# Attention steps for two heads at a time, diagonal blocks turned in two halves, and elementwise work on POOL

## The chip, the cores and the metric

The kernel runs on one core of a Trainium2 chip. The metric is the device time of one execution in microseconds (us). Before the change the median of three runs is 7115.45 us (7112.15 to 7116.17).

Engines are named as in the profile: PE (matmuls; PEld is its weight load), DVE and ACT (elementwise work and reductions, both read PSUM), POOL (elementwise work in SBUF, and indirect DMAs) and SP (which issues most DMAs). Each engine works through its own queue in order; semaphores tie the queues together.

## The reference, cut to what matters

```python
x = x + 0.5 * ffn(layernorm(x))       # mixture of 8 experts, top 2, on 16 x 1024 tokens of width 256
x = x + attn(layernorm(x))
x = x + 0.5 * ffn(layernorm(x))

def attn(x):                          # 16 batches, S = 1024, 16 heads of 16
    q = x @ W_q
    latent = (x @ W_k + x @ W_v) @ W_down_kv
    k, v = latent @ W_up_k, latent @ W_up_v
    scores = einsum('bhqd,bhkd->bhqk', q, k) / 16 * exp(-0.01 * abs(i - j))
    return (softmax(scores) @ v) @ W_o
```

## The kernel before, in words

The program is one expert layer (m1), the attention, and a second expert layer (m2). Only the attention (`class Attention`) is changed, so the functions of `Moe` stay as they are.

The attention takes 16 batches of 16 heads. Two heads make a pair (128 pairs, 8 per batch). A pair's scores are 1024 queries by 1024 keys for each head, and they are computed twice. First with queries on the partitions: `scores` (L933) fills half of four PSUM banks, `ps`, with 128 x 1024 scores of one head, and DVE takes the row maxima (L1193). The diagonal blocks need another decay, so at one place in eight (`DIAG`) DVE multiplies them by `Dm` into `Sd` instead (L1189), and a `fold` (L1198) takes their maxima. `max` (L1203, L1208) joins both into `m`, which goes through PE (`mturn`, L1004), ACT (L1097, L1098), POOL (`mlo`, L1261) and two DMAs through DRAM (`msend`, L900, L904) into two extra rows of `qst`. POOL subtracts `m` from `Sd` (`sub`, L1256). Then the scores come a second time with keys on the partitions and the maximum already subtracted, a row-tile (128 keys) at a time: `turned` (L945) fills the two halves of the queries, all but the diagonal block, and a transposition of `Sd` (L1033) fills that block. Each half is one PSUM unit of 128 x 512, in one of three banks (4 to 6) that all such units share in rotation; ACT takes the exponential into `P` (L1117), and `W` (L1049) multiplies it by V into bank 7, for four units at once in four column groups of the array. `P` has 8 slots, that is two row-tiles of both heads.

The operands of L933 and L945 are 48 and 50 rows high, head 0 on partitions 0 and up, head 1 on 64 and up. Score pieces of one head and turned pieces of the other are issued alternately, so that the two halves of the array work side by side. The transposition L1033 uses all 128 rows.

`order` writes the sequence in which all engines work. A step is one head of one row-tile; scores run ahead of the turned ones by one pair and `LEAD` steps. Between the steps it places the work of two lists: `late` (`norm`, `share`, and at a batch's end `oturn`, `out`, `sum`) and `ahead`, the next batch's preparation: `gather` (8 indirect DMAs, L1238), `add` (gate times expert row plus residual, L1146), `keep`, `stats`, `newton`, `center` (L1178), `turn`, `latent`, then 8 times `project` (L989, L992), `scale` (POOL L1245), `hi` (ACT L1088), `lo` (POOL L1250), `send` (two DMAs of `hl` to DRAM, L883), and `values` (L999). `stack` (L895) is 12 DMAs that build the operands of a pair, five row-tiles ahead of its first scores. Before the first `stack` of a new batch all that is left of `ahead` is written out in one go. In both programs that is the last three to four projections and all `values`.

## Time and profile before

| what | value |
|---|---|
| median of three runs | 7115.45 us |
| the profiled execution | 7060.19 us, its span 7057.4 us, granted clock 0.881 |
| PE busy | 5820.4 us (82%) |
| DVE busy | 4581.6 us (65%) |
| ACT busy | 3500.0 us (50%) |
| POOL busy | 2204.4 us (31%) |

The span is that of one execution under the profiler. The shares are means over three stages: in the attention, which is the long middle part of the 40 slices, PE stands at 8 to 9 tenths, DVE at 6 to 7, ACT at 5 to 6 and POOL at 2 to 3. In the slices of the expert layers, and in the gathers at both ends, the engines stand in other proportions; the change doesn't reach these.

### The profile page before, as it was taken

To read this page: it belongs to the slowest core of one execution; us is meant where nothing else is said; L and a number is where in the kernel's file an instruction comes from. 1 tells how busy PE (TensorE), PEld (TensorE's weight loads), DVE (VectorE), ACT (ScalarE), POOL (GpSimd) and SP (SyncE) were. 2 spreads that over 40 slices of the span, in tenths; PEclk is the share of its full clock that TensorE was granted. 3 is DMA by queue.
4 is the path that set the end of the run, shared out by engine and by line. 5 is a ranking of instruction groups with operands and counts; after the bars stand their busy time and mean duration, and the time that the engine had idled before them with its cause. 6 is when DMAs were issued, how large, how long until landed. Compare 5 with 4: busy or idle time off the path is not lost.

```text
span 7057.4 us, 109796 instructions
## 1 busy us (share of the span) xinstructions
PE 5820.4 (82%) x35596; PEld 3511.4 (50%) x35596; DVE 4581.6 (65%) x8862; ACT 3500.0 (50%) x7061; POOL 2204.4 (31%) x1732
## 2 busy tenths in 40 slices
PE   5499993898989888888898888988889885489992
PEld 5478882443444444444344343443434445478872
DVE  7555553766757667676676675757767667755574
ACT  1144441565556556665565555556556561134431
POOL 6700003233232332333323323233232216700066
PEclk9999995788889889998899988879989995589996
DMA  5433334454445544545445454444544424433387
GB/s 176 152 99 105 105 107 103 87 98 100 80 97 93 103 103 80 109 92 100 102 87 109 98 94 91 89 99 99 96 93 85 98 41 167 167 98 105 118 261 219
DMA packets 497051, 777.06 MB, mean 110 GB/s; under 512 B 77298, under 2 KB 373364, under 8 KB 471924
## 3 DMA queue, kind: packets, MB, share of 16 engines
q1 hardware_dynamic: 447348, 635.77, 40.1%
q0 software_dynamic: 49152, 134.28, 6.3%
q8 instruction: 305, 5.00, 0.3%
...
## 4 chain that ended last, share of the span: by engine, by line
PE 55%; DVE 13%; POOL 12%; issue 6%; ACT 6%; DMA 6%; SPq 1%; ACTq 0%; POOLq 0%; DVEq 0%
PE psum L933 11%; PE psum L1049 11%; PE psum L346 10%; POOL xs L617 7%; PE psum L1033 5%; DVE at_mx L1193 5%; PE psum L363 5%; PE psum L945 4%; ACT at_P L1117 4%; DMA parts<-at_hl 4%; POOL at_hl L1250 2%; DVE at_mab L1198 2%; PE psum L1023 2%; PE psum L989 2%; DVE at_XR L1146 2%
## 5 line engine op out<-in xcount | busy, mean ns | idle before, releaser
L1117 ACT ACTIVATE at_P<-psum 128x512 f32<-128x512 f32 x4096 | 2206.0, 596 | 1190.3 <-PE psum L945 1185.5
L1193 DVE TENSOR_REDUCE at_mx<-psum 128x8 f32<-128x1024 f32 x1792 | 2158.8, 1219 | 946.3 <-PE psum L933 942.6
L933 PE MATMUL psum<-at_kst,at_qst 48*128 48x128 f32 (+3 forms) x7168 | 1773.4, 365 | 150.2 <-DVE at_mx L1193 112.1
L945 PE MATMUL psum<-at_qst,at_kst 50*128 50x512 f32 (+3 forms) x5120 | 1540.9, 398 | 3.6 <-ACT at_P L1117 3.4
L933 PEld LDWEIGHTS psum<-at_kst,at_qst 48*128 48x128 f32 x7168 | 1116.8, 202 | 521.5 <-DVE at_mx L1193 184.3
L1049 PE MATMUL psum<-at_P,at_V 128*17 128x512 f32 x8192 | 1209.1, 663 | 0.0
L1256 POOL TENSOR_TENSOR at_Sd<-at_Sd,at_m 128x1024 f32<-128x1024 f32 x256 | 484.7, 1893 | 2091.7 <-DVE at_m L1208 2091.4
L1033 PEld LDWEIGHTS psum<-at_ident,at_Sd 128*128 128x128 f32 x2048 | 295.8, 144 | 1426.7 <-ACT at_P L1117 843.7
L1033 PE MATMUL psum<-at_ident,at_Sd 128*128 128x128 f32 x2048 | 695.5, 340 | 259.5 <-ACT at_P L1117 248.8
L945 PEld LDWEIGHTS psum<-at_qst,at_kst 50*128 50x128 f32 x5120 | 830.4, 199 | 15.1 <-ACT at_P L1117 9.8
L1189 DVE TENSOR_TENSOR at_Sd<-psum,at_Dm 128x1024 f32<-128x1024 f32 x256 | 312.7, 1222 | 572.1 <-PE psum L933 567.5
L1238 POOL DMA_INDIRECT at_xT<-ys,at_yib x256 | 243.5, 951 | 959.4 <-DMA at_gab<-table 710.6
L629 POOL DMA_INDIRECT m2Y<-ys,m2yi x256 | 246.1, 961 | 609.7 <-DMA ys<-m2X 500.1
L346 PE MATMUL psum<-m2wgu,m2xgT 128*128 x1632 | 429.0, 398 | 4.0 <-issue 3.2
L346 PE MATMUL psum<-m1wgu,m1xgT 128*128 x1584 | 416.0, 398 | 0.3 <-issue 0.3
L1245 POOL TENSOR_TENSOR at_qs<-at_qr,at_decay 128x1024 f32<-128x1024 f32 x128 | 302.9, 2366 | 353.2 <-ACT at_qr L1083 348.2
L1250 POOL TENSOR_TENSOR at_hl<-at_qs,at_hl 128x1024 fp32r<-128x1024 f32 x128 | 301.3, 2354 | 357.3 <-ACT at_hl L1088 357.3
L346 PEld LDWEIGHTS psum<-m2wgu,m2xgT 128*128 128x128 f32 x1632 | 289.1, 189 | 57.2 <-issue 8.4
L1198 DVE TENSOR_REDUCE at_mab<-at_Sd 128x8 f32<-128x1024 f32 x256 | 309.3, 1208 | 0.0
L346 PEld LDWEIGHTS psum<-m1wgu,m1xgT 128*128 128x128 f32 x1584 | 281.6, 190 | 49.9 <-issue 0.7
L562 DVE TENSOR_TENSOR m1X<-m1X,psum 128x256 f32<-128x256 f32 x264 | 111.0, 421 | 267.7 <-ACT m1X L396 267.7
L617 POOL DMA_INDIRECT xs<-m2X,m2idx x256 | 248.3, 970 | 108.7 <-issue 77.7
...
## 6 DMA issues: line engine op xcount, KB each, us to landing
parts<-at_hl SPq DMA_DIRECT2D x256, 512.0 KB, 3.9
...
```

What stands on the lines that cost most here:

```text
L346: ins = e.matmul(gu, self.xgT[:, j % 3, p, 128 * (k // 3):128 * (k // 3) + 128], self.wgu[q][:, k // 3, bass.ds(expert[j] * 512, 512)], st ...
L363: ins = e.matmul(bank[6 + i % 2][:, 0:D], self.hT[:, i % 2, p, 128 * (k // 3):128 * (k // 3) + 128], self.wdn[q][:, k // 3, bass.ds(expert ...
L617: e.indirect_dma_start(self.xs, bass.IndirectOffsetOnAxis(ap=self.idx[:, xb, t, k:k + 1], axis=0), self.X[:, xb, t, :], None).then_inc(sel ...
L933: ins = e.matmul(ps[:, 1024 * (z % 2) + col:1024 * (z % 2) + col + ln], self.qst[r:r + 48, s, side, 128 * t:128 * t + 128], self.kst[r:r + ...
L945: ins = e.matmul(bank[4 + a % 3][:, q0 - 512 * qh:q0 - 512 * qh + ln], self.kst[r:r + 50, s, side, 128 * kb:128 * kb + 128], self.qst[r:r ...
L1033: e.transpose(bank[4 + a % 3][:, 128 * (kb % 4):128 * (kb % 4) + 128], self.Sd[:, (2 * p + hh) % 4, kb, :], self.ident[:])
L1049: e.matmul(V[c:c + 17, :], self.V[:, b % 2, kb, 2 * (p % 8) + hh, :], self.P[:, self.p_slot(p, kb, hh, qh) % NP, :], start=(kb == 0), stop ...
L1117: e.activation(self.P[:, i % NP, :], bank[4 + a % 3], ACT.Exp).then_inc(self.taken.sem, 1)
L1193: e.tensor_reduce(self.mx[:, p % 2, hh, 8 * o:8 * o + 8], of, op=ALU.max, axis=AX.X).then_inc(self.s_read.sem, 1)
L1198: last_fold = own.end(e.tensor_reduce(self.mab[:, 1, 8 * (n % 2):8 * (n % 2) + 8], self.Sd[:, n % 4], op=ALU.max, axis=AX.X))
L1250: e.tensor_tensor(hl[:, :, 1, :], qs[:], hl[:, :, 0, :].bitcast(F32), ALU.subtract).then_inc(self.q_lo.sem, 1)
L1256: e.tensor_tensor(sd, sd, self.m[:, p % 2, 8 * hh:8 * hh + 8].rearrange("p (t o) -> p t o", o=1).to_broadcast([128, 8, 128]), ALU.subtract ...
```

## The change

Five things are changed, all in the attention.

- A step is now one row-tile for both heads (`order`, `step`). Between two row-tiles come `W` of the row-tile before, and up to two entries of the lists (before: one between any two steps). `LEAD` is 3 row-tiles, where it was 6 steps.
- The diagonal block is turned by two transpositions of 64 rows, `diagonal`: one ahead of the turned pieces, in the rows of this head, the other (`rest`) behind them, in the rows of the other head. The half with the diagonal block (near) is computed first, but stands second in the order of units: the half without it (far) is the first that ACT takes. `rest` waits on the semaphore `near` until the near pieces are done.
- `hl` has two buffers, and `hi` waits for the send before the last one.
- `add`, `center` and the multiplications of `share` go from DVE to POOL; `add` is a multiplication of 128 x 1024 and an addition of 128 x 1024 in place of four fused instructions of 128 x 256. The reciprocal of `share` stays on DVE.
- Both `fold`s of a pair stand behind both diagonal reads.

```diff
...
-    NS, NP, LEAD, DIAG = 3, 8, 6, 7
+    NS, NP, LEAD, DIAG = 3, 8, 3, 7
...
-        self.hl = sb("hl", [128, 2, 2, 512], F32R)
+        self.hl = sb("hl", [128, 2, 2, 2, 512], F32R)
...
+        for s in range(-8 - LEAD, 8 * NPAIR + 2):
+            p, kb = divmod(s, 8)
+            if kb == 0 and 2 <= p + 2 < NPAIR:
+                while ahead and ahead[0][0] <= (p + 2) // 8:
+                    yield from advance(ahead)
+                yield ("stack", p + 2)
+            z = s + 8 + LEAD
+            score = (z // 8, self.ORDER[z % 8]) if z < 8 * NPAIR else None
+            turn = (p, kb) if 0 <= s < 8 * NPAIR else None
+            if score or turn:
+                yield ("step", score, turn)
+            if score and score[1] == self.DIAG:
+                yield ("fold", score[0])
+            if score and z % 8 == 7:
+                yield ("max", score[0])
+                yield ("sub", 2 * score[0] + 1)
+            if 0 < s <= 8 * NPAIR:
+                wp, wk = divmod(s - 1, 8)
                 yield ("W", wp, wk)
                 if wk == 7:
                     late.append((wp, self.norm_order(wp)))
-            if s % 16 == 1 and 2 <= p + 2 < NPAIR:
-                while ahead and ahead[0][0] <= (p + 2) // 8:
-                    yield from advance(ahead)
-                yield ("stack", p + 2)
-            if late and (s % 2 == 0 or not ahead or s < 128 * (ahead[0][0] - 1)):
-                yield from advance(late)
-            elif ahead and s >= 128 * (ahead[0][0] - 1):
-                yield from advance(ahead)
-            z = s + 16 + LEAD
-            score = (2 * (z // 16) + z % 2, self.ORDER[z % 16 // 2]) if z < 16 * NPAIR else None
-            turn = (p, kb, 1 - half) if 0 <= s < 16 * NPAIR else None
-            if score or turn:
-                yield ("step", score, turn)
-            if folding:
...
+            if after and after[0][0] <= s:
+                p_max = after.pop(0)[1]
+                yield from (("mturn", p_max), ("mlo", p_max), ("sub", 2 * p_max), ("msend", p_max))
+            if score and z % 8 == 7:
+                after.append((s + 1, score[0]))
+            for turn_of in ((late, ahead), (ahead, late)):
+                queue = next((q for q in turn_of if q and (q is late or s >= 64 * (q[0][0] - 1))), None)
+                if queue:
+                    yield from advance(queue)
         for _b, items in late:
...
+                p, kb = item[2]
+                for hh in (1, 0):
+                    for qh in (1 - kb // 4, kb // 4):
+                        self.unit["T", p, kb, hh, qh] = len(self.unit)
...
-        return 32 * p + 4 * kb + 2 * (1 - hh) + qh
+        return 32 * p + 4 * kb + 2 * (1 - hh) + (qh ^ 1 - kb // 4)
...
+        def diagonal(p, kb, hh, r):
+
+            a, c = self.unit["T", p, kb, hh, kb // 4], 128 * (kb % 4)
+            return e.transpose(bank[4 + a % 3][:, c + r:c + r + 64], self.Sd[r:r + 64, (2 * p + hh) % 4, kb, :], self.ident[r:r + 64, r:r + 64])
+
...
+            s, r, d = p % NS, 64 * hh, kb // 4
+            far, near = (self.unit["T", p, kb, hh, qh] for qh in (1 - d, d))
             w.wait_ge(*self.m_rows[s].at(64 * (p // NS + 1)))
-            for qh in range(2):
-                a = self.unit["T", p, kb, hh, qh]
-                w.wait_ge(*self.taken.at(a - 2))
+            w.wait_ge(*self.taken.at(near - 2))
+            w.wait_ge(*self.shifted.at(2 * p + 2 - hh))
+            diagonal(p, kb, hh, r)
+            yield
+            for unit, qh in ((near, d), (far, 1 - d)):
                 runs = self.turned_pieces(kb, qh)
                 for q0, ln, side in runs:
-                    ins = e.matmul(bank[4 + a % 3][:, q0 - 512 * qh:q0 - 512 * qh + ln], self.kst[r:r + 50, s, side, 128 * kb:128 * kb + 128],
+                    ins = e.matmul(bank[4 + unit % 3][:, q0 - 512 * qh:q0 - 512 * qh + ln], self.kst[r:r + 50, s, side, 128 * kb:128 * kb + 128],
                                    self.qst[r:r + 50, s, 1 - side, q0:q0 + ln], start=True, stop=True)
                     if q0 == runs[-1][0]:
-                        ins.then_inc(self.filled.sem, 1)
+                        ins.then_inc(self.near.sem if unit == near else self.filled.sem, 1)
                     yield
+
+        def rest(p, kb, hh):
+
+            w.wait_ge(*self.near.at(16 * p + 2 * kb + 2 - hh))
+            diagonal(p, kb, hh, 64 - 64 * hh).then_inc(self.filled.sem, 1)
         z = 0
...
+                for hh in range(2):
+                    work = ([scores(2 * score[0] + hh, score[1], z + hh)] if score else []) + ([turned(*turn, 1 - hh)] if turn else [])
+                    if turn and hh:
+                        rest(*turn, 1)
+                    while work:
+                        work = [g for g in work if next(g, 1) != 1]
...
-                    p, kb, hh = turn
-                    a = self.unit["T", p, kb, hh, kb // 4]
-                    w.wait_ge(*self.shifted.at(2 * p + 2 - hh))
-                    w.wait_ge(*self.taken.at(a - 2))
-                    e.transpose(bank[4 + a % 3][:, 128 * (kb % 4):128 * (kb % 4) + 128], self.Sd[:, (2 * p + hh) % 4, kb, :], self.ident[:])
...
+                    rest(*turn, 0)
+                z += 2 if score else 0
...
-                w.wait_ge(*self.parts_out.at(32 * j))
-                e.activation(self.hl[:, :, 0, :], self.qs[:], ACT.Copy).then_inc(self.q_hi.sem, 1)
+                w.wait_ge(*self.parts_out[j % 2].at(32 * (j // 2)))
+                e.activation(self.hl[:, j % 2, :, 0, :], self.qs[:], ACT.Copy).then_inc(self.q_hi.sem, 1)
...
+                p, kb = at[1]
+                for hh in (1, 0):
+                    for qh in (1 - kb // 4, kb // 4):
+                        i, a = self.p_slot(p, kb, hh, qh), self.unit["T", p, kb, hh, qh]
+                        w.wait_ge(*self.filled.at(a + 1))
+                        w.wait_ge(*self.weighed.at(i - NP + 1))
+                        e.activation(self.P[:, i % NP, :], bank[4 + a % 3], ACT.Exp).then_inc(self.taken.sem, 1)
...
+            if kind == "add":
+                b, half, k = at
+                w.wait_ge(*self.y_in.at(128 * (2 * b + half + 1)))
+                y = self.rows.rearrange("p (t k) d -> p t k d", k=2)[:, :, k]
+                x = self.XR[:, 4 * half:4 * half + 4]
+                got = own.end(e.tensor_tensor(y, y, self.gab[:, 4 * half:4 * half + 4, k:k + 1].to_broadcast([128, 4, D]), ALU.mult))
+                w.wait_ge(*got)
+                ins = e.tensor_tensor(x, x, y, ALU.add)
+                if k:
+                    ins.then_inc(self.added.sem, 1)
+                else:
+                    w.wait_ge(*own.end(ins))
+            if kind == "center":
+                b, t = at
+                w.wait_ge(*self.spread.at(b + 1))
+                w.wait_ge(*self.x1_out.at(16 * (b + 1)))
+                ins = e.tensor_scalar(self.XR[:, t, :], self.XR[:, t, :], self.mv[:, t, 0:1], self.rs[:, t:t + 1], ALU.subtract, ALU.mult)
+                if t == 7:
+                    ins.then_inc(self.normed.sem, 1)
+            if kind == "share":
+                p = at[0]
+                on = self.On[:, p % 2].rearrange("p (t h q x) -> p t h q x", t=4, h=2, q=2)
+                w.wait_ge(*self.inverse.at(p + 1))
+                if p >= 8:
+                    w.wait_ge(*self.full("oturn", p // 8 - 1, 1, 1))
+                for qh in range(2):
+                    ins = e.tensor_tensor(self.OT[:, 4 * qh:4 * qh + 4, 32 * (p % 8):32 * (p % 8) + 32].rearrange("p t (h x) -> p t h x", h=2),
+                                          on[:, :, :, qh, 0:16], self.rc[:].rearrange("p t (h q) -> p t h q", q=2)[:, :, :, qh:qh + 1].to_broadcast([128, 4, 2, 16]),
+                                          ALU.mult)
+                ins.then_inc(self.shared.sem, 1)
             if kind == "scale":
...
-                e.tensor_tensor(hl[:, :, 1, :], qs[:], hl[:, :, 0, :].bitcast(F32), ALU.subtract).then_inc(self.q_lo.sem, 1)
+                e.tensor_tensor(hl[:, j % 2, :, 1, :], qs[:], hl[:, j % 2, :, 0, :].bitcast(F32), ALU.subtract).then_inc(self.q_lo.sem, 1)
...
```

PE, in the middle of a pair, before: `W` (L1049), one head's step (L1033 transposition of `Sd`, L933 scores, L945 turned), and the start of the next.

```order
L1049 MATMUL psum<-at_P,at_V 17x512 x4
L1033 MATMUL psum<-at_ident,at_Sd 128x128 [waits a_taken]
L933 MATMUL psum<-at_kst,at_qst 128x512 [waits a_s_read]
L945 MATMUL psum<-at_qst,at_kst 128x128
L933 MATMUL psum<-at_kst,at_qst 128x512
L945 MATMUL psum<-at_qst,at_kst 128x256
L945 MATMUL psum<-at_qst,at_kst 128x512 [waits a_taken]
L1033 MATMUL psum<-at_ident,at_Sd 128x128 [waits a_taken]
L933 MATMUL psum<-at_kst,at_qst 128x384 [waits a_s_read]
L945 MATMUL psum<-at_qst,at_kst 128x256
```

And now, from the end of the first head's half of a row-tile: the second half of the diagonal block (L946 with `a_near`), the other head, `W` (L1067), and the next row-tile.

```order
L946 MATMUL psum<-at_ident,at_Sd 128x64 [waits a_near]
L939 MATMUL psum<-at_kst,at_qst 128x128 [waits a_s_read]
L946 MATMUL psum<-at_ident,at_Sd 128x64 [waits a_taken]
L939 MATMUL psum<-at_kst,at_qst 128x384
L959 MATMUL psum<-at_qst,at_kst 128x384
L939 MATMUL psum<-at_kst,at_qst 128x512
L959 MATMUL psum<-at_qst,at_kst 128x512
L946 MATMUL psum<-at_ident,at_Sd 128x64 [waits a_near]
L1067 MATMUL psum<-at_P,at_V 17x512 x4
L939 MATMUL psum<-at_kst,at_qst 128x512 [waits a_s_read,a_stacked2]
L946 MATMUL psum<-at_ident,at_Sd 128x64 [waits a_taken]
L939 MATMUL psum<-at_kst,at_qst 128x384
```

What was a full-height transposition ahead of every step is now two 64-row ones in the run of row-tiled matmuls, and `W` stands behind both heads. Between the two heads there is nothing but the wait of the second `diagonal` on `a_taken`, ACT's count of units taken.

POOL, at the end of a batch's output, before: `sum` (L1266), the second gather (L1238), `sub` (L1256), `sum`, `mlo` (L1261), `sub`.

```order
L1266 TENSOR_TENSOR at_ob<-at_ob,at_res 128x512 [waits a_res_in1,a_taken]
L1238 DMA at_xT<-ys,at_yib 128x256 [waits a_added]
L1238 DMA at_xT<-ys,at_yib 128x256 x7
L1256 TENSOR_TENSOR at_Sd<-at_Sd,at_m 128x1024 [waits a_m_max]
L1266 TENSOR_TENSOR at_ob<-at_ob,at_res 128x512 [waits a_res_in0,a_taken]
L1261 TENSOR_TENSOR at_mp<-at_mT,at_mp 16x128 [waits a_taken]
L1256 TENSOR_TENSOR at_Sd<-at_Sd,at_m 128x1024
```

And now: the two `add`s (L1237, L1239) first, and the gather behind `sub` (L1278) and `sum` (L1288), straight ahead of `mlo` (L1283).

```order
L1237 TENSOR_TENSOR at_xT<-at_xT,at_gab 128x4x256 [waits a_y_in]
L1239 TENSOR_TENSOR at_XR<-at_XR,at_xT 128x1024 [waits pool_steps]
L1237 TENSOR_TENSOR at_xT<-at_xT,at_gab 128x4x256 [waits pool_steps]
L1239 TENSOR_TENSOR at_XR<-at_XR,at_xT 128x1024 [waits pool_steps]
L1278 TENSOR_TENSOR at_Sd<-at_Sd,at_m 128x1024 [waits a_m_max]
L1288 TENSOR_TENSOR at_ob<-at_ob,at_res 128x512 [waits a_res_in0,a_taken]
L1230 DMA at_xT<-ys,at_yib 128x256 [waits a_added]
L1230 DMA at_xT<-ys,at_yib 128x256 x7
L1283 TENSOR_TENSOR at_mp<-at_mT,at_mp 16x128 [waits a_taken]
L1278 TENSOR_TENSOR at_Sd<-at_Sd,at_m 128x1024
```

The gather has moved from ahead of the maximum's `sub` to between it and `mlo`.

## Rows read from the trace of the kernel before

**Rows 1.** Busy time by stretch: the attention, and one burst of preparation at a batch's end.

```profile
core 0: us, PE busy (x) PEld busy (x) DVE busy (x) ACT busy (x) POOL busy (x), PEclk, DMA share, GB/s
1233.00:5814.00 4581.00, 3990.89 (x24737) 1929.02 (x24737) 3105.41 (x3604) 2733.70 (x5154) 1392.78 (x915) 0.89 0.48 93
2609.00:2634.00 25.00, 15.11 (x43) 7.68 (x42) 1.95 (x2) 8.54 (x14) 14.38 (x7) 0.53 0.34 126
```

**Rows 2.** Waits from 1500 to 5500 us: who waits for whom, us, times, longest.

```profile
PEld psum L1033 <- ACT at_P L1117: 728.3, 860, 2.8
ACT at_hl L1088 <- DMA parts<-at_hl: 195.0, 43, 7.0
```

**Rows 3.** Timeline of PE: `W` of six row-tiles in a row.

```profile
2660.87 1.05 PE L1049 MATMUL psum<-at_P,at_V 128*17 128x512 f32 x8
2664.12 1.05 PE L1049 MATMUL psum<-at_P,at_V 128*17 128x512 f32 x8
2667.76 1.05 PE L1049 MATMUL psum<-at_P,at_V 128*17 128x512 f32 x8
2670.88 1.09 PE L1049 MATMUL psum<-at_P,at_V 128*17 128x512 f32 x8
2674.78 1.58 PE L1049 MATMUL psum<-at_P,at_V 128*17 128x512 f32 x8
2679.73 1.91 PE L1049 MATMUL psum<-at_P,at_V 128*17 128x512 f32 x8
```

**Rows 4.** Timeline of all engines: a step from its transposition to the next one.

```profile
2525.34 0.33 PE L1033 MATMUL psum<-at_ident,at_Sd 128*128 128x128 f32 x1
...
2525.60 0.50 PE L945 MATMUL psum<-at_qst,at_kst 50*128 50x512 f32 x1
...
2525.98 0.39 PE L933 MATMUL psum<-at_kst,at_qst 48*128 48x512 f32 x1
2526.13 1.09 ACT L1117 ACTIVATE at_P<-psum 128x512 f32<-128x512 f32 x2 [0.88 <-PE psum L945]
...
2526.78 0.33 PE L1033 MATMUL psum<-at_ident,at_Sd 128*128 128x128 f32 x1 [0.41 <-ACT at_P L1117]
```

**Rows 5.** Groups by line and shape, 1500 to 5500 us: busy, mean ns of one.

```profile
L1033 PE MATMUL psum<-at_ident,at_Sd 128*128 128x128 f32 x1770 | 599.7, 339 | 227.8 <-ACT at_P L1117 217.6
L1256 POOL TENSOR_TENSOR at_Sd<-at_Sd,at_m 128x1024 f32<-128x1024 f32 x222 | 420.0, 1892 | 1755.8 <-DVE at_m L1208 1755.5
L1250 POOL TENSOR_TENSOR at_hl<-at_qs,at_hl 128x1024 fp32r<-128x1024 f32 x108 | 254.3, 2355 | 296.9 <-ACT at_hl L1088 296.9
L1238 POOL DMA_INDIRECT at_xT<-ys,at_yib x224 | 212.6, 949 | 233.3 <-DVE at_XR L1146 164.8 <-issue 68.5
L1146 DVE SCALAR_TENSOR_TENSOR at_XR<-at_xT,at_gab,at_XR 128x256 f32<-128x256 f32 x224 | 114.1, 569 | 0.0
L1266 POOL TENSOR_TENSOR at_ob<-at_ob,at_res 128x512 f32<-128x512 f32 x56 | 71.2, 1271 | 90.0 <-ACT at_ob L1111 90.0
```

**Rows 6.** Timeline around one `add`, DVE and POOL.

```profile
2493.68 1.89 POOL L1256 TENSOR_TENSOR at_Sd<-at_Sd,at_m 128x1024 f32<-128x1024 f32 x1
2493.86 3.18 DVE L1146 SCALAR_TENSOR_TENSOR at_XR<-at_xT,at_gab,at_XR 128x256 f32<-128x256 f32 x4
2498.10 1.66 DVE L1146 SCALAR_TENSOR_TENSOR at_XR<-at_xT,at_gab,at_XR 128x256 f32<-128x256 f32 x4
```

**Rows 7.** Timeline of ACT, POOL and PE in the burst of rows 1.

```profile
2621.87 1.06 ACT L1088 ACTIVATE at_hl<-at_qs 128x1024 fp32r<-128x1024 f32 x1 [6.47 <-DMA parts<-at_hl]
2625.49 2.34 POOL L1245 TENSOR_TENSOR at_qs<-at_qr,at_decay 128x1024 f32<-128x1024 f32 x1
2629.89 1.06 ACT L1088 ACTIVATE at_hl<-at_qs 128x1024 fp32r<-128x1024 f32 x1 [6.48 <-DMA parts<-at_hl]
...
2633.48 0.47 PE L1033 MATMUL psum<-at_ident,at_Sd 128*128 128x128 f32 x1
```

**Rows 8.** Timeline of one pair's maximum on its way into `qst`, and the pair's first scores' wait.

```profile
2652.49 0.17 DVE L1208 TENSOR_TENSOR at_m<-at_mab 128x16 f32<-128x16 f32 x1
2652.97 0.49 PE L933 MATMUL psum<-at_kst,at_qst 48*128 48x512 f32 x1 [1.35 <-DMA at_qst<-parts]
2656.86 0.45 POOL L1261 TENSOR_TENSOR at_mp<-at_mT,at_mp 16x128 fp32r<-16x128 f32 x1 [2.22 <-ACT at_mT L1098]
2658.76 1.16 SPq L904 DMA_DIRECT2D at_qst<-mdram  x4
```

108 lines of the change are left out of this document (30 added, 78 removed).

## The prediction

> **What bounds the kernel now.** I read the busy time by stretch first, since the page's shares mix three stages. Attention, the only stage that changes, takes 4581 of 7057 us for 1024 row-tiles, 4.47 us each; in it PE is busy 3991 us, DVE 3105, ACT 2734, POOL 1393, and the granted clock is 0.89 [rows 1]. No engine is full, so a chain through several sets the pace. The waits name it: PE's weight loads for the transposition of `Sd` wait 728 us for ACT's exponential [rows 2]. In the timeline, `W` to `W`, row-tiles take 3.25, 3.64 (with a `norm` inside), 3.12 and 3.90 us (with the multiplications of `share` behind a fold); where the clock is at its lower level, 1.2 GHz, `W` itself takes 1.91 instead of 1.05 us and the row-tile 4.95 [rows 3]. Less 0.5 for `norm`, the first four average 3.35.
>
> Inside a step [rows 4]: the transposition starts at 2525.34, the turned pieces 0.26 later, the first unit is ready at 2526.10, ACT starts at 2526.13, and the next transposition at 2526.78, 0.65 after that, having idled 0.41 for ACT. The last piece starts at 2525.98 and ends at 2526.37, so a step costs PE 0.97 without waits. PE alone would need 2 x 0.97 + 1.0 for `W` = 2.94 per row-tile. The rest, some 0.4, is the exponential between two steps that have no `W` between them, and DVE.
>
> **The row-tile.** The change takes away two changes of the array's shape per row-tile, with their transpositions (339 ns each [rows 5]), and adds four transpositions of 64 columns and two waits of PE on itself. PE's own need falls: two steps without the 0.26 are 2 x 0.71, and with `W` it is 2.4. But the exposed exponential stays. The second `diagonal` waits until the first head's far unit is taken. That unit is ready after the diagonal (about 0.05), the near pieces (384 columns, 0.16) and the far piece (0.50, as the 512 piece of [rows 4]): 0.7. ACT's start and the exponential add 0.03 + 0.65, so the second head starts 1.4 after the first. It needs 0.05 + 0.16 + 0.21 of streaming, the rest of the diagonal and 0.1 of turn-over: 0.7. Then `W`, 1.0. Sum 3.1. No row shows `rest` or its wait: it costs nothing if it hides behind the far piece (0.21), and at most a transposition after a wait, 0.33 [rows 4], twice, so 3.0 to 3.7; I take 3.1, since the far piece does run behind the near one. To this come 0.75 + 0.3 per pair: DVE's two folds now come in one block, and in the row-tile with eight score pieces the second head is late. (8 x 3.1 + 1.05) / 8 = 3.24 against 3.35: 0.11 x 1024 = **-110 us**, from +350 to -360.
>
> The Trainium skill (TensorEngine Tiling, Key Properties) says that switching the tiling mode, not the tile, drains TensorE. The trace agrees, with 0.26 us ahead of the first turned piece [rows 4]. By that rule alone the change is worth three switches a row-tile; the sum above does without it, because it counts what ACT lets through. It returns as a rival.
>
> **Longer work in the lists.** Before, some of it stood between the steps where PE idles 0.41 anyway [rows 4]. Now all of it stands behind `W`, where PE doesn't wait, and nothing stands between the heads. Eight projections, two `latent` and four `out` per batch are 14; half of 0.41 each, over 16 batches, is **+45 us** (0 to +90).
>
> **The clock.** A step at 1.2 GHz loses less when there are fewer of its parts: 0.89 granted [rows 1] means 2 x 0.11 x 4581 = 1008 us at the lower level, and a row-tile there takes 4.95 [rows 3]; 0.4 less of 5 is 8%, on the half that is not bursts: **-40 us** (+60 to -150, as more or less time falls there).
>
> **The second `hl`.** In the burst `hi` waits 6.47 and 6.48 us for the send, and the cycle from one `hi` to the next is 8.02 [rows 7]. With two buffers it is bound by POOL and ACT: `scale` 2.34 + `hi` 1.06 + `lo` 2.36 [rows 5, 7] and hand-overs of 0.05 each = 5.9. But the burst now holds one projection more: from its first `hi` to its last are 3.4 + 2 x 5.9 + 2.4 = 17.6 us, where it was some 19 from ACT's last exponential (2611) to 2629.89. I take 1.5 for that, the work that has left the row-tiles (a `hi` of 1.06 and a projection) 1.5, and 1 for the waits outside, since nearly all of the 195 us in 14 batches, 14 each, lie in the burst [rows 2, 7]: 4 x 15 = **-60 us** (-20 to -150). Behind the burst the next pair's first scores wait 1.35 us for the stack already [rows 8]; that comes from DMA, which isn't faster now, so five quicker row-tiles give back 1 us per batch: **+15**. Preparing the first batch gains 8 x 2.1 in this chain and loses 11 in `add` and `center`: **-6**.
>
> **POOL.** Two-operand work costs it 1271 ns for 512 columns and 2355 for 1024, so 0.19 + 2.12 ns a column; with one operand spread out, 1892 [rows 5]. One `add` is then 1.89 + 2.36 + 0.15 = 4.4 us, four a batch 17.6. A `center` is between 0.19 + 256 x 1.67 ns = 0.62 and, if its two scalars per partition cost it more, 1.0; I take 0.62, eight are 5. On DVE one half's adds took 3.18 + 1.66 us [rows 6], 9.7 a batch, of which PE loses about 8.
>
> Where this is late now, per batch, measured from `m`:
> - The gather is 8 x 0.95 = 7.6 us [rows 5] and stands between `sub` and `mlo`. `mlo` started at 4.4 [rows 8]; now 1.9 + 1.3 + 7.6 = 10.8, L904 1.9 later, its four issues 1.2 and the landing 1.4 (what is left of the 1.9 between `mlo` and L904): 15.3. PE wants the rows after three row-tiles, an `out` and an `mturn`: 11. It waits 4.3.
> - `stats` waits on DVE for the last `add`: POOL does `sub`, `share`, `mlo`, `sub` (5.9) and two `add`s: 14.7. DVE is there after three row-tiles, 9.4. It waits 5.3, and behind it stand the score reads that PE waits for.
> - `turn` waits for `center`: 1.9 + 5.0 = 6.9 against 3.0. PE waits 3.9.
>
> Together 13.5 against 8: 5.5 x 15 = **+85 us** (-60, if the slack of the chain holds most of it, to +200, with `center` at 1.0 and each wait followed by a lower clock).
>
> The Trainium skill (SBUF, "SBUF: two separate sides") says that a DVE operation with two inputs in SBUF and a POOL operation lock each other out of one port pair, the first holding it to its end. The trace bears it out: four adds take 3.18 us beside `sub` and 1.66 alone [rows 6]. The rule speaks for moving them; against it, POOL holds the pair some 24 us more per batch, and the join of the maxima (L1208) has two SBUF inputs. At most 2.4 us in a few pairs would not change the sum.
>
> **Sum.** -110 +45 -40 -60 +15 -6 +85 = -71 on the profiled execution's 7060, so 6989. The median of the runs is 55 above that execution: **7044 us**, 1.0% less.
>
> **Rivals.**
> - *PE's own time decides.* If the wait for ACT shrinks with the switches, because the far unit is ready much earlier than 0.7, the row-tile goes to what DVE allows: 3105 us [rows 1] less adds, centres and shares (some 250) is 2.8 per row-tile; 0.5 x 1024 = -510, so 6600 to 6750. For it: PE has 0.5 less to do, and DVE and ACT have room. Against it: the same exponential in the same three banks ends the wait [rows 4]. 0.14. The Trainium skill's rule on switches, taken alone, would have it so.
> - *The queue of POOL decides* (slower). Besides the three places above, every pair's maximum must now cross POOL, two DMAs and PE within three quicker row-tiles. With `mturn` behind `W`, `mlo` ends 4.0 after `m`; the rows land 4.1 later (1.45 to L904, 1.2 of issues, 1.4 of landing [rows 8]), at 8.1, and are wanted at 9.1, three row-tiles and an `mturn` on. If `share`, `lo` or a send takes 2.5 us more, PE waits 1.5 in each of 128 pairs, +190, and the quicker row-tile is given back to it: 7044 + 190 = 7234 with all pairs, 7170 if two in three are met. It decides once the chain from `m` is longer than 9.1. For it: the slack is 1 us, and the trace has `mlo` start at 4.4, not 3.6 [rows 8]. Against it: most pairs have nothing else on POOL. 0.22.
> - *`rest` is exposed* (slower). Each costs 0.33: +0.5 per row-tile, and the sum is +300 with some of it under ACT's time: 7200. 0.10.
> - *Nothing moves.* The row-tile comes out at 3.3, and the rest cancels: 7100 to 7130. 0.12.
> - The forecast, 7044 within 60 or so: 0.42.
>
> A measurement of this kernel can tell 0.2%, 14 us, from no change. Faster holds the forecast but for a tenth, and the first rival: 0.55. Same 0.11. Slower 0.34. The range from 6840 to 7220 leaves out most of the first rival and the far end of the second, 0.2 in all.
>
> **What would show it.** Right: `W` to `W` 3.0 to 3.2 at full clock; the second L946 of a row-tile idle about 0.6 for ACT `at_P`; no wait of L1106 for `parts`; hi to hi 5.9 in the burst; PE idle 4 us for L904's rows once a batch, DVE idle 5 us at L1156 for POOL, PE 4 us at the first `turn`. Wrong: `W` to `W` below 2.9 or above 3.4, `rest` starting more than 0.1 after the last score piece, or those three waits under 1 us.

## The result, and the profile after

| | before | after |
|---|---|---|
| median | 7113.8 us (7111.11 to 7116.17, 4 runs) | 7689.56 us (7662.98 to 7698.43, 4 runs) |
| profiled execution: span, granted clock | 7057.4 us, 0.881 | 7693.5 us, 0.811 |
| PE, DVE busy | 5820.4, 4581.6 us | 6200.0, 4395.1 us |
| ACT, POOL busy | 3500.0, 2204.4 us | 3581.2, 2729.1 us |

The changed kernel is 8% slower: 1.0803 [1.0775, 1.0831]. 7044 us was predicted, within 6840 to 7220. The sign was wrong.

The attention as one stretch of the changed kernel (columns as in [rows 1]: length, then busy us of PE, PEld, DVE, ACT, POOL with instructions, granted clock, DMA share, GB/s):

```profile
1237.00:6447.00 5210.00, 4368.93 (x26781) 2169.49 (x26779) 2924.80 (x2988) 2813.07 (x5154) 1888.05 (x1408) 0.79 0.42 82
```

It was 4581 us at 0.89, so it accounts for 629 of the 636 us that the span grew. PE is busy 378 us longer, although the change takes work from it, and idle 841 instead of 590 us. At 0.79, 2 x 0.21 x 5210 = 2190 us lie at 1.2 GHz; it was 1008. (Counted stretch by stretch in the record of the granted clock they are 2216 and 995.) `W` to `W` in plain row-tiles, from the same kernel's PE timeline (start, length):

```profile
3137.09 1.05 PE L1067 MATMUL psum<-at_P,at_V 128*17 128x512 f32 x8
3140.56 1.05 PE L1067 MATMUL psum<-at_P,at_V 128*17 128x512 f32 x8
3143.82 1.05 PE L1067 MATMUL psum<-at_P,at_V 128*17 128x512 f32 x8
3147.23 1.05 PE L1067 MATMUL psum<-at_P,at_V 128*17 128x512 f32 x8
...
3157.30 1.91 PE L1067 MATMUL psum<-at_P,at_V 128*17 128x512 f32 x8
3162.23 1.91 PE L1067 MATMUL psum<-at_P,at_V 128*17 128x512 f32 x8
3167.26 1.91 PE L1067 MATMUL psum<-at_P,at_V 128*17 128x512 f32 x8
3172.37 1.91 PE L1067 MATMUL psum<-at_P,at_V 128*17 128x512 f32 x8
```

Inside the row-tile from 3140.56 to 3143.82, the starts of the first and the second head:

```profile
3141.55 0.27 PE L946 MATMUL psum<-at_ident,at_Sd 64*128 64x64 f32 x1
3143.06 0.27 PE L946 MATMUL psum<-at_ident,at_Sd 64*128 64x64 f32 x1 [0.38 <-ACT at_P L1137]
```

At full clock a row-tile takes 3.26 to 3.47 us here, 3.38 on average; at 1.2 GHz it takes 4.93 to 5.11. The row-tiles at full clock are about as long as before's [rows 3], and far fewer are at full clock. With 3.3 and 5.03 us for a row-tile at the two levels, the 1180 us more at 1.2 GHz cost an estimated 1180 x (1 - 3.3 / 5.03) = 405 us of the 629. Of the other 224 most must be waits, since PE is idle 251 us longer. First those of PE from 1500 to 6000 us, then DVE's (who waits for whom, us, times, longest):

```profile
PE psum L946 <- ACT at_P L1137: 285.2, 691, 2.5
PE psum L992 <- POOL at_XR L1248: 115.2, 14, 8.6
PE psum L1018 <- ACT at_qr L1101: 106.9, 26, 4.3
PE psum L946 <- DMA at_qst<-mdram: 89.8, 14, 7.0
...
PE psum L1018 <- ACT at_V L1111: 50.9, 13, 3.9
```

```profile
DVE at_st L1163 <- POOL at_XR L1239: 71.0, 14, 5.1
```

PEld's waits hold the wait of `rest` for the near pieces, 0.28 us on average, in 1042 of the 1750 heads that these 4500 us hold:

```profile
PEld psum L946 <- PE psum L959: 296.4, 1042, 0.6
```

POOL's groups, 1500 to 5500 us (busy, mean ns of one), show what the moved work costs there:

```profile
L1248 POOL TENSOR_SCALAR at_XR<-at_XR,at_mv,at_rs 128x256 f32<-128x256 f32 x96 | 115.6, 1210 | 8.8 <-DVE at_rs L1180 8.8
L1239 POOL TENSOR_TENSOR at_XR<-at_XR,at_xT 128x1024 f32<-128x1024 f32 x48 | 113.6, 2367 | 3.8
L1237 POOL TENSOR_TENSOR at_xT<-at_xT,at_gab 128x1024 f32<-128x1024 f32 x48 | 90.9, 1893 | 1.9
```

And in the burst, ACT's `hi` no longer waits for the parts [rows 7]; it waits for POOL:

```profile
2760.59 1.06 ACT L1106 ACTIVATE at_hl<-at_qs 128x1024 fp32r<-128x1024 f32 x1 [4.45 <-POOL at_qs L1267]
2766.57 1.06 ACT L1106 ACTIVATE at_hl<-at_qs 128x1024 fp32r<-128x1024 f32 x1 [4.45 <-POOL at_qs L1267]
2772.56 1.06 ACT L1106 ACTIVATE at_hl<-at_qs 128x1024 fp32r<-128x1024 f32 x1 [4.45 <-POOL at_qs L1267]
```

### The profile page after: what moved, and what is told of

Same layout as the page of the kernel before. It is cut to its first block, busy times and chain, and to the rows that moved or that the text cites. A ratio compares the mean times of both kernels' runs of the same rounds, so it can differ in the third digit from the quotient of the medians.

```text
span 7693.5 us, 114239 instructions
## 1 busy us (share of the span) xinstructions
PE 6200.0 (81%) x37644; PEld 3756.1 (49%) x37644; DVE 4395.1 (57%) x8222; ACT 3581.2 (47%) x7061; POOL 2729.1 (35%) x2244
## 4 chain that ended last, share of the span: by engine, by line
PE 57%; POOL 20%; issue 11%; ACT 7%; DVE 4%; DMA 1%; SPq 0%; POOLq 0%; ACTq 0%; DVEq 0%
PE psum L1067 13%; PE psum L346 9%; PE psum L959 9%; PE psum L939 8%; POOL xs L617 6%; ACT at_P L1137 5%; PE psum L363 5%; PE psum L946 5%; POOL at_qs L1267 3%; POOL at_hl L1272 2%; POOL at_XR L1248 2%; PE psum L1042 2%; POOL at_Sd L1278 1%; PE psum L335 1%; PE psum L354 1%
## 5 line engine op out<-in xcount | busy, mean ns | idle before, releaser
L1137 ACT ACTIVATE at_P<-psum 128x512 f32<-128x512 f32 x4096 | 2230.6, 595 | 1422.7 <-PE psum L959 1340.2
L939 PE MATMUL psum<-at_kst,at_qst 48*128 48x128 f32 (+3 forms) x7168 | 2138.8, 415 | 91.5 <-DVE at_Sd L1189 58.5
L939 PEld LDWEIGHTS psum<-at_kst,at_qst 48*128 48x128 f32 x7168 | 1266.0, 225 | 921.5 <-issue 437.1
L959 PE MATMUL psum<-at_qst,at_kst 50*128 50x512 f32 (+3 forms) x5120 | 1690.3, 433 | 0.0
L946 PE MATMUL psum<-at_ident,at_Sd 64*128 64x64 f32 x4096 | 1207.8, 296 | 448.5 <-ACT at_P L1137 337.8
L1067 PE MATMUL psum<-at_P,at_V 128*17 128x512 f32 x8192 | 1360.5, 743 | 0.0
L946 PEld LDWEIGHTS psum<-at_ident,at_Sd 64*128 64x128 f32 x4096 | 609.7, 149 | 1135.7 <-ACT at_P L1137 624.5
L959 PEld LDWEIGHTS psum<-at_qst,at_kst 50*128 50x128 f32 x5120 | 1033.7, 255 | 0.0
L1278 POOL TENSOR_TENSOR at_Sd<-at_Sd,at_m 128x1024 f32<-128x1024 f32 x256 | 484.2, 1891 | 1226.0 <-DVE at_m L1209 1226.0
L1258 POOL TENSOR_TENSOR at_OT<-at_On,at_rc 128x128 f32<-128x128 f32 x256 | 98.5, 406 | 1524.0 <-DVE at_rc L1214 1524.0
(245 smaller groups left out, 7693.5 us busy)
```

The source lines that it names most:

```text
L939: ins = e.matmul(ps[:, 1024 * (z % 2) + col:1024 * (z % 2) + col + ln], self.qst[r:r + 48, s, side, 128 * t:128 * t + 128], self.kst[r:r + ...
L946: return e.transpose(bank[4 + a % 3][:, c + r:c + r + 64], self.Sd[r:r + 64, (2 * p + hh) % 4, kb, :], self.ident[r:r + 64, r:r + 64])
L959: ins = e.matmul(bank[4 + unit % 3][:, q0 - 512 * qh:q0 - 512 * qh + ln], self.kst[r:r + 50, s, side, 128 * kb:128 * kb + 128], self.qst[r ...
L1067: e.matmul(V[c:c + 17, :], self.V[:, b % 2, kb, 2 * (p % 8) + hh, :], self.P[:, self.p_slot(p, kb, hh, qh) % NP, :], start=(kb == 0), stop ...
L1137: e.activation(self.P[:, i % NP, :], bank[4 + a % 3], ACT.Exp).then_inc(self.taken.sem, 1)
L1278: e.tensor_tensor(sd, sd, self.m[:, p % 2, 8 * hh:8 * hh + 8].rearrange("p (t o) -> p t o", o=1).to_broadcast([128, 8, 128]), ALU.subtract ...
```

## The experiments

Eighteen kernels ran on five chips, A to E, and the kernel before ran beside them on each: it took 7102 us (median) on A, and 7551, 7572, 7573 and 7510 on B to E. A ratio is to the kernel before on the same chip. Ratios shift between chips too: the changed kernel was 1.080 at first and 1.056 on D. The traces show where most of the difference lies. On D the changed kernel's attention is as long as at first, 5212 and 5210 us; its expert layers take 1309 + 1455 us and not 1237 + 1246. The second of them, first chip and D (columns as in [rows 1]):

```profile
6447.00:7693.00 1246.00, 907.76 (x5428) 789.43 (x5428) 772.54 (x2750) 378.63 (x951) 500.97 (x518) 0.80 0.50 161
```

```profile
6521.00:7976.00 1455.00, 953.25 (x5432) 810.12 (x5428) 769.84 (x2750) 370.00 (x951) 496.37 (x518) 0.77 0.43 138
```

The kernel before was not profiled on B to E. From its granted clock there, 0.845 to 0.862, less the time at 1.2 GHz outside the attention that e8 and e11 show (some 850 us), I estimate that 27 to 29% of its attention lie at 1.2 GHz on these chips, not 22%. So close comparisons are made on one chip, and the share of a kernel of B to E is held against 28%. The last columns are of the stretch from 1600 to 5600 us of the profiled execution, which is attention in all kernels: row-tiles done (instructions of `W` by 8) and the share of time at 1.2 GHz, twice what the granted clock lacks to 1.

| chip | kernel | ratio to before | row-tiles in 4000 us | at 1.2 GHz |
|---|---|---|---|---|
| first | before | 1 | 879 | 22% |
| first | changed | 1.0803 [1.0775, 1.0831] | 776 | 42% |
| A | e1, POOL's three back on DVE | 1.0735 [1.0676, 1.0794] | 783 | 48% |
| A | e2, only `center` back | 1.0595 [1.0544, 1.0646] | 801 | 36% |
| A | e3, whole transpositions | 1.0522 [1.0459, 1.0585] | 802 | 28% |
| A | e4, before, three on POOL | 1.0015 [0.9990, 1.0041] | 871 | 24% |
| B | e5, two heads a step, second `hl` | 1.0230 [1.0172, 1.0289] | 819 | 32% |
| B | e6, before, halves | 1.0358 [1.0296, 1.0420] | 798 | 42% |
| B | e7, changed, more columns | 1.0739 [1.0685, 1.0794] | 753 | 40% |
| B | e8, before, second `hl` | 0.9876 [0.9799, 0.9953] | 851 | 28% |
| C | e9, changed, 2048 whole ones added | 1.2641 [1.2575, 1.2708] | 600 | 70% |
| C | e10, changed, waits partly filled | 1.0653 [1.0605, 1.0702] | 757 | 40% |
| C | e11, before, far unit first | 1.0099 [1.0058, 1.0139] | 820 | 28% |
| C | e12, before, second `hl`, POOL | 0.9826 [0.9791, 0.9861] | 858 | 24% |
| D | e13, changed, 1024 added behind `W` | 1.0653 [1.0595, 1.0710] | 763 | 36% |
| D | e14, the same, a piece later | 1.2324 [1.2250, 1.2398] | 619 | 74% |
| D | e15, changed again | 1.0561 [1.0508, 1.0614] | 772 | 42% |
| D | e16, e12, 1024 added behind `W` | 0.9953 [0.9923, 0.9983] | 844 | 24% |
| E | e17, halves in the whole one's place | 1.1472 [1.1402, 1.1541] | 685 | 62% |
| E | e18, e3 again | 1.0421 [1.0357, 1.0486] | 795 | 30% |

**e1 and e2: is it POOL?** `add`, `center` and the multiplications of `share` go back to DVE (e1), or `center` alone (e2).

```diff
-                e.tensor_tensor(rs[:], rs[:], sq[:], ALU.mult).then_inc(self.spread.sem, 1)
+                last = own.end(e.tensor_tensor(rs[:], rs[:], sq[:], ALU.mult))
+            if kind == "center":
...
```

> The changed kernel with add, center and the multiplications of share back on DVE. Theory A (POOL's in-order queue makes the three waits per batch, and the lower clock that follows them is all the rest): the loss goes nearly whole, 7100 to 7200 us. Theory B (the row-tile of two heads itself leaves the array longer at 1.2 GHz): only the waits of about 19 us per batch against some 8 of the DVE work go, and the lower clock behind them, 200 to 270 us: 7420 to 7500, with plain row-tiles still at the lower clock far from any wait.

> The changed kernel with only center back on DVE. center took 1.21 us on POOL and PE waited 8.6 us for it in each of 15 batches. Theory A: 8.6 and the 9 us at the lower clock behind it (a third of these lost) go, less 2 us of DVE work: 15 x 10 = 150, so 7540. Theory B: the same 100 to 150 here; it differs from A only in that the share of lower clock elsewhere stays (about 2000 us of 5200).

e1 is 1.0735, 0.007 under the changed kernel and, with both intervals, at most 0.015, across two chips; at 7618 us it lies above what either theory allowed. e2 is 1.0595, better than e1, which moves more back, and its 7531 us are what both theories expected; e1 also spent more time at 1.2 GHz. Why `add` or `share` on DVE should cost clock was not settled.

**e3: whole transpositions.** The changed kernel with one 128-row transposition ahead of each head; the far unit is computed first, nothing waits on near pieces.

```diff
-            return e.transpose(bank[4 + a % 3][:, c + r:c + r + 64], self.Sd[r:r + 64, (2 * p + hh) % 4, kb, :], self.ident[r:r + 64, r:r + 64])
+            e.transpose(bank[4 + a % 3][:, 128 * (kb % 4):128 * (kb % 4) + 128], self.Sd[:, (2 * p + hh) % 4, kb, :], self.ident[:])
...
-                rest(*turn, 0)
```

> The changed kernel with the diagonal block turned by one transposition of 128 rows ahead of each head, the far unit computed first and no wait of PE on itself. Theory A: the form of the diagonal costs next to nothing, 7650 to 7750. Theory B, with the halves as its cause: the lower clock shrinks to what it was before and the time falls to 7350 to 7450. Theory B with the order of the two heads as its cause: within 60 us of 7690.

**e4: POOL's part in the structure of before.**

> The kernel before with only add, center and the multiplications of share on POOL. Theory A: it carries most of the loss, 7400 to 7600. Theory B: the waits of POOL's queue less the DVE work, 150 to 200 us: 7270 to 7320.

e3 takes off 0.028, and time at 1.2 GHz falls from 42 to 28%: the halves, with their order and their wait, are a third of the loss (e18, below, makes it less). Over the attention it is 1421 us at 1.2 GHz against 2216, and 995 in before, so the halves account for 795 of the 1221 us more; the rest of the added time at 1.2 GHz came with the other parts. e4 is no different from before, where both theories had it slower: DVE, relieved of 243 us in the 4000 (2707 to 2464), was not what set the pace there.

**e5 to e8: each part alone.** e5 is e3 with the three operations on DVE, and a gather held back while a pair's maximum is under way. e6 is before with the halves, the order of units and the wait of the change. e8 is before with the second `hl`. e7 is the changed kernel with one score piece of the first head written twice:

```diff
+            if n % 2 == 0:
+                ins = e.matmul(ps[:, 1024 * (z % 2) + col:1024 * (z % 2) + col + ln], ...)
```

> The changed kernel with the 128-row transposition, with add, center and share on DVE, and with a gather held back while a maximum is between max and msend: what is left of the change are the two heads to a row-tile and the second hl. Theory P (the parts add up, each with its own waits and clock): e3 minus the center's 8.6 and the gather's 6.3 us of waits per batch, 7489 - 15 x 20 = about 7190, near the kernel before. Theory Q (the two heads to a row-tile cost by themselves): 7300 or more.

> The kernel before with only the diagonal block turned in two halves, one head at a time as before. Theory P' (the halves lower the array's activity, so that it stays at 1.2 GHz for longer after every wait): low-clock time in the attention up from 995 to 1500 us or more, 7250 to 7400. Theory Q' (the halves do harm only in the row-tile of two heads): 7000 to 7130, since two changes of shape per row-tile are gone.

> The changed kernel with the last score piece of the first head of each row-tile computed twice over (same values): 128 to 512 more columns for PE per row-tile, in the place where it waits for ACT. If activity of the array in plain row-tiles decides how long it stays at 1.2 GHz, low-clock time falls well below 2213 us and the time below 7600. If not, it costs 0 to 0.2 us in 1024 row-tiles: 7690 to 7890.

> The kernel before with only the second buffer of hl. The burst's cycle falls from 8.02 to about 5.9 us for three projections per batch: 15 x 6 = 90 us less, and 17 in the first batch: 7000 to 7030. If what is behind the burst waits for the stack anyway, 7090.

The halves with their order and wait cost 0.036 in the structure of before (e6). Two heads a step cost 0.035 (e5 less e8), in which the new order of units, the place of the `fold`s and the gather held back are included. e5 falls between its two expectations, e6 and e8 came as the first of theirs. The second `hl` gives 0.012 (e8). One more score piece per row-tile, 128 to 512 columns on 48 rows, doesn't bring the clock back (e7, 40%); the changed kernel was not run on B, so what the piece costs can't be told.

**e9 to e12.** e9 adds a whole transposition ahead of each head's first half, which the halves then write over:

```diff
             w.wait_ge(*self.shifted.at(2 * p + 2 - hh))
+            e.transpose(bank[4 + near % 3][:, 128 * (kb % 4):128 * (kb % 4) + 128], self.Sd[:, (2 * p + hh) % 4, kb, :], self.ident[:])
             diagonal(p, kb, hh, r)
```

e10 adds, ahead of the wait for a bank, transpositions of a constant into `ps` where PE idles longest:

```diff
+                if kind == "turn" and at[1] + at[2] == 0:
+                    fill(24)
+                if kind == "values" and at[1] < 3:
+                    fill(12)
                 w.wait_ge(*self.taken.at(a - 2))
```

> The changed kernel with one more PE instruction per head and row-tile: a whole 128-row transposition of the diagonal block, ahead of the two halves, which then write the same block again (2048 more instructions; in the kernel before such a one shows about 0.3 us, mostly beside other work, a half in the changed kernel 0.27 to 0.30). Theory (the time lost is TensorE's clock, and what took the clock away is that no operation over all 128 rows is left in a plain step): time at the lower clock falls from 2213 us of the attention to below 1700, full-clock row-tiles grow from 3.3 to 3.4 us, and the whole is 1 to 3% under the changed kernel, 1.05 to 1.07 of before. Rival (the halves cost through their order and their wait on the near unit, not through their shape): the added work only adds, 1.08 to 1.10, lower-clock time 2200 us or more.

> The changed kernel with transpositions of a constant on PE where it waits longest: 24 (about 6 us) ahead of the first turn of a batch, where PE waits 8.6 us for the last center, and 12 (about 3 us) ahead of each of the first three values of a batch, where it waits 4 us each for ACT. They write a half of ps that the next scores overwrite. Theory (long waits of PE take the clock away, and the row-tiles behind them pay for it): the two low stretches behind these places get shorter, lower-clock time falls by 200 to 600 us, the time by 1 to 3%. Rival (the clock is lost in the plain row-tiles themselves, by what their instructions are): within 0.7% of the changed kernel, or slower by the part of the fillers that doesn't fit the waits (up to 14 x 3 us, 0.6%); lower-clock time stays at 2100 to 2300 us.

> The kernel before with the order of the units alone: of each head's two units the one without the diagonal block comes first; the block is turned by one 128-row transposition ahead of the step, as in before, and nothing waits on near pieces. Against the kernel with the halves (1.036 of before) it tells the order from the shape. Theory (the 64-row halves and their wait cost the clock): 0.995 to 1.005 of before, lower-clock time about 1000 to 1300 us. Rival (the order costs: the unit that ACT takes first is now the one without the transposition, so the banks come free otherwise): 1.02 to 1.04, lower-clock time near 2000.

> The kernel before with two of the five parts: the second buffer of outgoing parts and add, center and the multiplications of share on POOL. Each alone gave 0.988 [0.980, 0.995] and 1.0015 [0.999, 1.004]. Theory (a shorter burst, everything else as before, DVE's relief worth nothing): 0.985 to 0.995. Rival (the 0.988 was the other chip's lower clock, not the buffer): 0.998 to 1.005. A third: the center's wait on POOL is exposed once the burst is shorter, 1.00 to 1.01.

e9 missed both expectations by far: 2048 instructions of some 0.3 us, 0.6 ms at most one after the other, put 1.4 to 1.6 ms on the changed kernel (1.264 against 1.056 to 1.080), and 70% of the stretch is at 1.2 GHz. e10 leaves that share at 40%, but it did not fill the waits: PE's longest for POOL fell from 8.6 to 4.7 us, and all its waits for POOL, `at_qr` and `at_V` from 273 to 178 us. That long waits are not what sets the changed kernel apart is better seen in e18, which has the same ones and 30% at 1.2 GHz. PE's wait for `center` in the changed kernel on D (e15), in e10, and in e18:

```profile
PE psum L992 <- POOL at_XR L1248: 100.3, 13, 8.6
```

```profile
PE psum L1002 <- POOL at_XR L1258: 54.9, 13, 4.7
```

```profile
PE psum L985 <- POOL at_XR L1239: 105.2, 14, 8.9
```

e11 falls between its two expectations: the order of units costs 0.010, at the share that before is estimated to have there. e6 less e11, across two chips, leaves 0.026 for the halves themselves and their wait. e12 beats both kernels.

**e13 to e16: place.** e13 adds 1024 whole transpositions, one per row-tile, directly behind `W`; e14 the same ones behind the first score piece of the row-tile, which stands on 48 rows.

```diff
                 if turn:
+                    extra(*turn, 1)
                 for hh in range(2):
```

> The changed kernel with one whole 128-row transposition per row-tile more (1024 in all), directly behind W; the halves write the same block again. Theory (TensorE's clock comes back after stretches of PE without idle time in which operations over all 128 rows stand side by side, as W and the transposition did in before; the halves took that away): time at the lower clock falls below 1700 us of the attention (the changed kernel 2213), and the time stays at or under the changed kernel's of the same call, though 1024 x 0.3 us are added. Rival (any such operation costs more than it gives, as 1.264 for two per row-tile shows): 0.1 to 0.2 of before above the changed kernel, as for the one a piece later.

> The same 1024 instructions as in the kernel with the transposition directly behind W, one instruction later: behind the first score piece of the row-tile, which stands on 48 rows. Theory: 0.08 to 0.14 of before above the changed kernel, lower-clock time over 2800 us. Rival (the place makes no difference): within 0.02 of the kernel with it directly behind W.

> The changed kernel as it is, for its ratio and its lower-clock time on the chip of this call. The chips differ, so 1.07 to 1.09 of before is expected, as it was on the first (1.080).

> The kernel before with the second buffer of parts and the three operations on POOL (0.983 of before), in which the transposition directly behind W is done twice: 1024 x 0.27 us more at full clock. Theory: the lower-clock time falls from 1145 to 600 to 900 us, which gives back 100 to 180 us of some 200 added; 0.985 to 1.01 of before. Rival (the clock doesn't depend on it, or falls with any added operation): lower-clock time 1200 us or more, 1.01 to 1.05.

Instructions and data are the same in e13 and e14; the times are 8072 and 9326 us. e14 is 0.176 above the changed kernel on the same chip (e15), more than the 0.08 to 0.14 expected. The same stretch of the two, `W` alone (busy us and instructions of PE and of PEld, clock, DMA share, GB/s), e13 first:

```profile
1600.00:5600.00 4000.00, 971.89 (x6104) 105.55 (x6096) 0.82 0.42 84
```

```profile
1600.00:5600.00 4000.00, 1020.66 (x4952) 90.95 (x4952) 0.63 0.34 66
```

Row-tiles of e14 around a fall of the clock (PE timeline):

```profile
3063.10 1.05 PE L1077 MATMUL psum<-at_P,at_V 128*17 128x512 f32 x8
3067.08 1.91 PE L1077 MATMUL psum<-at_P,at_V 128*17 128x512 f32 x8
3073.63 1.91 PE L1077 MATMUL psum<-at_P,at_V 128*17 128x512 f32 x8
3079.66 1.91 PE L1077 MATMUL psum<-at_P,at_V 128*17 128x512 f32 x8
3086.02 1.91 PE L1077 MATMUL psum<-at_P,at_V 128*17 128x512 f32 x8
```

At full clock a row-tile is 3.98 us, against 3.46 in e13 (3062.26 to 3065.72): the score piece stands alone where it ran beside turned pieces. Then it is 6.0 to 6.6 at 1.2 GHz, and it stays there in these rows. So part of what e14 costs is the place itself, at either clock: its attention is 1255 us longer than e13's, and the 2829 us more at 1.2 GHz account for an estimated 2829 x (1 - 3.98 / 6.03) = 960 of them. e13 is 0.009 over e15, though its instructions are 1024 x 0.26 = 266 us, 0.035: most comes back, with 36% instead of 42% at 1.2 GHz. "Below 1700 us" at the lower clock was not reached (counted over the attention, 1943). e15 itself, at 1.056, is below the 1.07 to 1.09 that was expected; its expert layers are longer, and its attention is not. e16 has the time that its theory gave and not the mechanism, so it speaks against the wider reading: in before's structure, where a whole transposition stands behind `W` already, a second gives no clock back (24% both) and costs 0.013.

**e17 and e18: shape or place.** e17 has e3's order, with the half in the other head's rows where e3 has its whole transposition, and the own half first among the turned pieces.

```diff
-            e.transpose(bank[4 + a % 3][:, 128 * (kb % 4):128 * (kb % 4) + 128], self.Sd[:, (2 * p + hh) % 4, kb, :], self.ident[:])
+            half(p, kb, hh, 64 - 64 * hh).then_inc(self.near.sem, 1)
...
+            w.wait_ge(*self.near.at(16 * p + 2 * kb + 2 - hh))
+            half(p, kb, hh, r)
```

> The changed kernel in which the half of the diagonal block in the other head's rows stands ahead of each head's pieces, the other half first among the turned pieces, and the far unit is computed first: the place of the 128-row transposition that gave 1.052 on the first chip, with the shape of the change. It waits on the other half before its own instead of on the near pieces at the end. Theory (it is the shape: with halves no 128-row operation stands beside W, and TensorE's clock stays low longer): within 0.01 of the changed kernel (1.056 on the second chip), lower-clock time over 1900 us of the attention. Rival (it is the place: halves behind the near pieces, and the wait for these at the end of every head): within 0.01 of the kernel with whole transpositions, lower-clock time about 1400 to 1600 us.

> The changed kernel with whole 128-row transpositions ahead of each head, as on the first chip (1.052 there, the changed kernel 1.080), now on the chip of this call and beside the kernel with the halves at the same place. Expected 1.025 to 1.045 of before, lower-clock time about 1400 us.

It is the shape: at the same place halves cost 0.105 over a whole transposition. The rival is out, and the theory's figure too: halves there are far worse than the change's own. One thing comes with the shape in e17, the wait of the second half for the first; PE idles only 6.9 us for it from 1500 to 6000. Of the 813 us that e17's attention is longer than e18's, the 2124 us more at 1.2 GHz account for an estimated 2124 x (1 - 3.6 / 5.5) = 730, with e17's plain row-tiles, 3.6 us at full clock and 5.5 at 1.2 GHz. Against the changed kernel whole transpositions give back less here than on A: e18 is 0.014 under e15 and its attention 146 us shorter, where e3's was 202 us shorter than the changed kernel's. `W` alone in the same stretch, e17, then e18:

```profile
1600.00:5600.00 4000.00, 1045.21 (x5480) 98.97 (x5480) 0.69 0.37 74
```

```profile
1600.00:5600.00 4000.00, 961.59 (x6360) 108.72 (x6360) 0.85 0.44 86
```

What differs is how long the clock stays down, not how often it falls. Counted in the record of the granted clock over the attention, it falls 77 times in before, 97 in the changed kernel, 76 in e17, 109 in e18 and 88 in e14; its mean stay at 1.2 GHz is 13, 23, 47, 13 and 54 us. Rows of one place in each of two kernels show what stands behind `W` then; that it is so in all places was not looked into. In before, at 1.2 GHz, a whole transposition follows `W` at once; the piece behind it, 0.51 us for 512 columns and not 0.79, is already at the higher clock:

```profile
2502.20 1.91 PE L1049 MATMUL psum<-at_P,at_V 128*17 128x512 f32 x8
2504.04 0.47 PE L1033 MATMUL psum<-at_ident,at_Sd 128*128 128x128 f32 x1
2504.44 0.51 PE L933 MATMUL psum<-at_kst,at_qst 48*128 48x512 f32 x1
```

In the changed kernel pieces of 48 to 64 rows follow `W`, the second head waits 0.5 us for ACT, and the clock stays down for row-tile after row-tile:

```profile
3122.74 1.91 PE L1067 MATMUL psum<-at_P,at_V 128*17 128x512 f32 x8
3124.58 0.58 PE L939 MATMUL psum<-at_kst,at_qst 48*128 48x256 f32 x1
3124.58 0.36 PE L946 MATMUL psum<-at_ident,at_Sd 64*128 64x64 f32 x1
...
3126.52 0.36 PE L946 MATMUL psum<-at_ident,at_Sd 64*128 64x64 f32 x1 [0.50 <-ACT at_P L1137]
...
3127.67 1.91 PE L1067 MATMUL psum<-at_P,at_V 128*17 128x512 f32 x8
```

## Why the prediction was wrong, point by point

- **The clock, -40 us: the step that failed.** I took time at 1.2 GHz as given and only made its row-tiles shorter, with +60 as the worst. It more than doubled, 1008 to 2190 us, and cost an estimated +405. That is 445 of the 707 us between the sum's -71 and the +636 measured. The mechanism wasn't among the rivals either: with half-height transpositions in place of whole ones TensorE stays at 1.2 GHz longer once it is there. Shown by e18 against e17 (0.105), e3 against the changed kernel (795 us at 1.2 GHz) and e6 against before (0.036); e15 against e14 (0.176 for 1024 instructions in one place) shows that place matters as well. The other 426 us at 1.2 GHz came with two heads a step and POOL's work and weren't traced to one of them. Long waits are not what sets the changed kernel apart, since e18 has the same ones, and one more score piece per row-tile gives nothing (e7). Which property of these instructions the clock responds to is not settled: e16 shows that more 128-row work behind `W` doesn't always help.
- **The row-tile, -110 us.** In the row-tile from 3140.56 to 3143.82 `W` takes 0.99 us, the first head 1.51 and the second 0.76, where 1.0, 1.4 and 0.7 were predicted. So the terms were right in kind and each a little short: 3.1 us predicted, 3.26 to 3.47 measured, 3.38 on average, against 3.35 before. Nothing of the gain came. `rest` was costed at nothing and waits 0.28 us on average, mostly beside a piece of the other head. The Trainium skill's rule (TensorEngine Tiling, Key Properties) that a change of tiling mode drains TensorE, which would have made the change a gain by itself, is not refuted as to the drain, but it is the lesser effect: e6 does just that, removes the switches, and is 3.6% slower.
- **Sums that don't hold as written.** (8 x 3.1 + 1.05) / 8 is 3.23, so the row-tile's term is -120; with the 1.05 its upper end, 3.7, gives +490 and not +350. A step of [rows 4], from 2525.34 to 2526.37, is 1.03 and not 0.97. The rival "`rest` is exposed" adds 300 to 7044, which is 7344 and outside the range, not 7200. None of this turns the sign of the forecast.
- **Lists, +45, and two heads a step.** Not measured apart. e5 less e8 puts two heads a step, with the order of units and the held gather, at +0.035 in all, where my terms made it a gain. In e5 PE's transposition waits 447 us for ACT between 1500 and 6000, in e8 234. But e11, which has the new order of units alone and one head a step, waits 425, so it is the order that exposes the exponential oftener, and what two heads a step add beyond it is not shown by these waits. Some of the 0.035 is clock (32 against 28%).
- **The second `hl`, -60 us.** Right in mechanism and near in size: hi to hi 5.98 us against 5.9 predicted, no wait for parts, and e8 gives 0.988 [0.980, 0.995], which is 35 to 150 us.
- **The stack, +15, and the first batch, -6.** The first row-tiles stand at 1237 us and stood at 1233, so the first batch lost 4 us. The stack was not measured apart; e8 holds it as far as the second buffer sets it.
- **POOL, +85 us.** Two of three waits were too small: the first `turn` waits 8.2 us (115.2 in 14) and not 3.9, since a `center` takes 1.21 and not 0.62 us; the extra 8 x 0.59 is 4.7. The rows of the maximum wait 6.4 (89.8 in 14), 4.3 predicted; `stats` waits 5.1, 5.3 predicted. As a whole the part is small: e4 costs nothing, e1 gives back 0.007, at most 0.015.
- **SBUF's ports.** The port rule of the Trainium skill (SBUF, "SBUF: two separate sides") spoke for moving `add` off DVE, and I gave it no weight in the sum. e4, with `add` on POOL, is 1.0015, so nothing was won by it.
- **The rivals.** "The queue of POOL decides" had the right sign, but its times, 7170 to 7234, are some 450 us short, and e1 and e4 refute its mechanism. "`rest` is exposed" had 0.10 and named the right instructions for another reason. "PE's own time decides" had it upside down: PE's time grew, by its clock.

The Trainium skill (TensorE: Matmul & The Clock Gate, A second HAM failure mode: psum-queue depth-cycling) describes a clock that falls when PE idles a little between groups of matmuls again and again. The changed kernel's small waits of PE for ACT, 0.41 us on average, fit it. But e18 has more of them with 30% of the time at 1.2 GHz, and e17 fewer with 62%; so they don't explain the difference. From 1500 to 6000 us, e18, then e17:

```profile
PE psum L948 <- ACT at_P L1128: 444.4, 763, 4.3
```

```profile
PE psum L948 <- ACT at_P L1135: 323.2, 693, 2.4
```
